# bf16 operands for the LayerNorm sums of the feed-forward phase in a two-layer transformer kernel

## The chip, the cores and the metric

The kernel runs on all 8 NeuronCores of one Trainium2 chip (trn2). Each core does the same program on its own batch element, with no exchange between cores, so there is one launch and eight equal shares. The metric is the device time of the slowest core in microseconds (us). TensorE (PE) does matmuls, VectorE (DVE) and ScalarE (ACT) do element-wise work and read the matmuls' results, SyncE (SP) and GpSimd (POOL) issue the DMAs. The engines run side by side and meet at semaphores.

## The reference, cut to what matters

For each of 8 batch elements, x is 4096 tokens by 1024 features. Two pre-norm layers are applied:

```python
x = x + attn0(layernorm(x))    # 16 heads, causal, sigmoid instead of softmax
x = x + ffn0(layernorm(x))     # silu(x @ wg.T) * (x @ wu.T) @ wd.T, hidden 3072, weights int / 127
x = x + attn1(layernorm(x))    # one head, band of 256, layernorm on its output
x = x + ffn1(layernorm(x))     # activations rounded to 8 bits, ternary weights

def _layernorm(x, axis=-1, eps=1e-5):
    m = jnp.mean(x, axis=axis, keepdims=True)
    v = jnp.var(x, axis=axis, keepdims=True)
    return (x - m) / jnp.sqrt(v + eps)
```

The change touches the mean and the variance of the layernorm in the second line.

## The kernel before

The four lines above are four phases, one after the other, with a barrier between them; they hand x on through DRAM. All of x is kept feature-major: 1024 features are 8 chunks of 128 partitions, and the 4096 tokens lie along the free axis. Phase 2 is `emit_p2`. It first loads and converts its three weight matrices, then loops over 8 blocks of 512 tokens (`NT2 = 8`, `W2 = 512`, `NDC = 8` chunks).

`emit_stats` computes a block's mean and variance. Since the features lie along the partitions, the sum over them is a matmul with a column of ones: for each of the 8 chunks ACT squares the chunk (`AF.Square`, line 96 by the helper `act`), PE adds the chunk to a row of sums and its square to a second row (both recorded at line 76, the helper `mm`). Then a few operations on one row of 512 follow: four on DVE (the first writes `r_mean`), Ln and Exp on ACT, one more on DVE. Two matmuls with a row of ones spread the two rows over 128 partitions (`ab`, `bb`). `emit_apply` multiplies by `ab` into the f32 scratch `self.sq` (shown as `sqb` in the profile) and adds `bb`, giving the normalized block in bf16, 16 DVE operations (line 123 by the helper `tt`).

`emit_stats` has two forms. Without `cast_bufs`, the sums are f32 matmuls that read x itself and an f32 square in `self.sq`. With `cast_bufs`, DVE first casts each chunk to bf16 (helper `vcopy`, line 128), ACT writes the square as bf16, and the two matmuls are bf16 with a bf16 column of ones. Each of the two scratch pairs is used in turn, and the cast and the square of chunk i wait for the matmul of chunk i - 2. Phases 1, 3 and 4 use the second form with buffers of their own; phase 2 uses the first. SBUF in phase 2 is mostly taken by the weights.

The order in each engine's queue is the order of the program text, since every engine runs its list in order. In phase 2 that is: `stage(0)` (load, statistics, apply of block 0), then for each block the 24 hidden tiles (8 gate matmuls, 8 up matmuls, Silu on ACT, product on DVE), then `stage(tc + 1)`, the statistics and the apply of the next block, then the 8 down tiles of this block. Each down tile is 24 matmuls into the one PSUM bank `Y`, and an add of the residual tile `p_xres` on DVE which also frees the bank for the next down tile; so the first such add stands behind the 16 apply operations in DVE's queue. The residual tiles and the next block of x are loaded by SP, the results stored by POOL.

Of the kernel before, what the change touches and what calls it, by code (L numbers as in the profile page):

```python
# [7 lines left out]
BF16 = mybir.dt.bfloat16  # L8
# [166 lines left out]
class Builder:  # L175
# [392 lines left out]
    def emit_p2(self):  # L568
        nc, p, d = self.nc, self.plan, self.d
        gd, sc, ve, pe = self.gd, self.sc, self.ve, self.pe  # L570
# [75 lines left out]
        src_r = src.rearrange("(c p) t -> p c t", p=128)  # L646
        dst_w = dst.rearrange("(c p) t -> p c t", p=128)

        apply_of = {}
        store_done = {}  # L650
        sil_done = {}
# [4 lines left out]
        def stage(tcn):  # L656
            lds = self.lxA
            prev_apply = apply_of.get(tcn - 1, 0)
            if tcn == 0:
                nld = tc0_ld  # L660
            else:
                p.dma("sync", x1col.ap().rearrange("p (c j) -> p c j", c=NDC),
                      src_r[:, :, tcn * W2:(tcn + 1) * W2],
                      waits=[(ve, prev_apply)], inc=lds)
                nld = lds.n
            bc = self.emit_stats(
                lambda i, b=x1col: b[:, i * W2:(i + 1) * W2], W2, NDC,
                ab, bb, [(lds, nld)],
                war_bank=[(ve, prev_apply)] if prev_apply else [])
            apply_of[tcn] = self.emit_apply(  # L670
                lambda dc, b=x1col: b[:, dc * W2:(dc + 1) * W2],
                lambda dc: xn1[:, dc * W2:(dc + 1) * W2],
                W2, NDC, ab, bb, bc)

        stage(0)
        for tc in range(NT2):
            apply_done = apply_of[tc]
# [29 lines left out]
            if tc + 1 < NT2:  # L707
                stage(tc + 1)
# [523 lines left out]
```

How the kernel before makes its waits and increments, by code:

```python
            def section(e, _ops=ops):  # L162
                for fn, wl, inc, by in _ops:
                    for s, v in wl:
                        e.wait_ge(s.h, v)
                    if fn is None:
                        continue
                    ins = fn(e)
                    if inc is not None:
                        ins.then_inc(inc.h, by)
```

## Time and profile before

| | us |
|---|---|
| median of the two timed runs | 5796.78 |
| the two runs | 5672.54, 5921.03 |
| the profiled execution | 5667.68 |
| its span on the slowest core (core 6) | 5666.1 |
| spans of the eight cores | 5641.7 to 5666.1 |

The mean granted clock of TensorE is 0.727 to 0.732 of full speed on all eight cores in the profiled execution. Phase 2 has its first matmul on x at 2063 us and its last at about 3596 us; the first 200 us of that are the loading and the conversion of the weights. Times in the rows below are us from the start of the span, unless marked ns. In a timeline row the first number is the start, the second the time from the first start to the last end of so many instructions (x2 is two of them), and the bracket gives how long the engine sat idle before it and which instruction's end let it go on. The f32 matmuls leave two records each.

### The profile page before, as it was taken

To read this page: it belongs to the slowest core of one execution; us is meant where nothing else is said; L and a number is where in the kernel's file an instruction comes from. 1 tells how busy PE (TensorE), PEld (TensorE's weight loads), DVE (VectorE), ACT (ScalarE), POOL (GpSimd) and SP (SyncE) were. 2 spreads that over 40 slices of the span, in tenths; PEclk is the share of its full clock that TensorE was granted. 3 is DMA by queue.
4 is the path that set the end of the run, shared out by engine and by line. 5 is a ranking of instruction groups with operands and counts; after the bars stand their busy time and mean duration, and the time that the engine had idled before them with its cause. 6 is when DMAs were issued, how large, how long until landed. Compare 5 with 4: busy or idle time off the path is not lost.

```text
span 5666.1 us, 48803 instructions; the slowest of 8 cores (5641.7 to 5666.1 us)
## 1 busy us (share of the span) xinstructions
PE 3582.7 (63%) x14626; PEld 1346.6 (24%) x14770; DVE 1871.3 (33%) x4451; ACT 1743.1 (31%) x1790; POOL 86.1 (2%) x150
## 2 busy tenths in 40 slices
PE   3376666766766720898888898456565556345554
PEld 0011111211111100333333333123333223111211
DVE  5613222132132210222222212134444444465555
ACT  2175665755756631211111111011111222011111
POOL 0000000000000000000000000000000000000000
PEclk6576765666767665899999999777777677556566
DMA  3100000000000054011110010400000000101010
GB/s 89 45 1 30 30 1 30 0 30 30 1 30 30 1 128 102 19 45 45 45 43 17 31 44 30 102 1 31 31 31 31 31 31 15 45 30 60 30 60 30
DMA packets 71534, 206.60 MB, mean 36 GB/s; under 512 B 5746, under 2 KB 9842, under 8 KB 69234
## 3 DMA queue, kind: packets, MB, share of 16 engines
q1 hardware_dynamic: 47474, 112.24, 6.3%
q0 software_dynamic: 23808, 91.24, 5.2%
q8 instruction: 129, 2.11, 0.2%
q14 instruction: 123, 1.01, 0.1%
HBM read 152.08 MB, written 67.11 MB: 39 GB/s over the span
## 4 chain that ended last, share of the span: by engine, by line
PE 50%; DVE 22%; ACT 14%; issue 8%; DMA 5%; DVEq 1%; ACTq 0%; SPq 0%; POOL 0%; POOLq 0%
PE pW L76 33%; PE p L76 12%; ACT p_ate L96 6%; ACT p_ato L96 5%; DVE sqb L123 3%; DVE p_xn L123 3%; PE pW L86 2%; PE p L86 2%; DVE p_ato L123 1%; DVE p_ate L123 1%; DVE p_osb L128 1%; DMA p_wq<-wqkv 1%; DMA p_wl<-w0d 1%; DVEq L165 1%; DMA p_wl<-w0g 1%
## 5 line engine op out<-in xcount | busy, mean ns | idle before, releaser
L76 PE MATMUL pW<-p_xn,p_kc 64*128 64x512 bf16 x2304 | 698.1, 502 | 287.4 <-ACT p_ato L96 142.5
L96 ACT ACTIVATE p_ate<-pW 128x1536 bf16<-128x1536 f32 (+2 forms) x408 | 560.9, 1375 | 600.7 <-PE pW L76 582.5
L96 ACT ACTIVATE p_ato<-pW 128x1536 bf16<-128x1536 f32 (+2 forms) x408 | 561.0, 1375 | 41.9 <-PE pW L76 8.1
L76 PE MATMUL p<-p_ate,p_vc 128*64 128x512 bf16 x1152 | 474.1, 544 | 135.9 <-DVE p_ato L123 135.7
L79 PE MATMUL p<-p_ato,p_vc 128*64 128x512 bf16 x1152 | 479.8, 543 | 9.0 <-ACT p_ato L96 8.2
L123 DVE TENSOR_TENSOR p_x1c<-p_xc,p 64x512 f32<-64x512 f32 x128 | 87.7, 685 | 1068.2 <-PE p L79 1061.2
L76 PE MATMUL p<-p_h,p_wd 128*128 128x512 bf16 x1504 | 369.3, 403 | 101.5 <-DVE p_xres L123 96.9
L76 PE MATMUL pW<-p_xn,p_wq 128*128 128x512 bf16 x1504 | 346.4, 392 | 128.1 <-DVE p_xn L123 93.9
L76 PE MATMUL pW<-p_xn,p_wg 128*128 128x512 bf16 x1504 | 361.4, 380 | 14.9 <-DVE p_xn L123 13.3
L76 PE MATMUL pW<-p_xn,p_wu 128*128 128x512 bf16 x1504 | 360.5, 379 | 1.7
L76 PEld LDWEIGHTS pW<-p_xn,p_kc 64*128 64x128 bf16 x2304 | 159.6, 106 | 802.2 <-issue 764.8
L123 DVE TENSOR_TENSOR p_h<-p_h,pW 128x512 bf16<-128x512 bf16 x192 | 132.1, 688 | 534.2 <-PE pW L76 509.7
L96 ACT ACTIVATE p_h<-pW 128x512 bf16<-128x512 f32 x192 | 114.6, 597 | 516.0 <-PE pW L76 515.9
L76 PEld LDWEIGHTS p<-p_ate,p_vc 128*64 128x64 bf16 x1152 | 126.0, 138 | 454.8 <-issue 441.8
L76 PEld LDWEIGHTS pW<-p_xn,p_wq 128*128 128x128 bf16 x1536 | 153.7, 100 | 329.4 <-issue 160.1
L76 PEld LDWEIGHTS p<-p_h,p_wd 128*128 128x128 bf16 x1536 | 153.3, 103 | 325.0 <-issue 176.7
L76 PE MATMUL pW<-p_xb,ones_b 128*1 128x512 bf16 x192 | 96.2, 501 | 196.0 <-DVE p_xb L128 194.6
L96 ACT ACT_TABLE_LOAD x19 | 24.4, 1283 | 584.3 <-PE pW L76 521.7
L76 PEld LDWEIGHTS pW<-p_xn,p_wg 128*128 128x128 bf16 x1536 | 150.5, 98 | 196.4 <-issue 16.1
L76 PEld LDWEIGHTS pW<-p_xn,p_wu 128*128 128x128 bf16 x1536 | 150.5, 98 | 182.0 <-issue 1.4
L76 PE MATMUL pW<-sqb,ones_col 128*1 128x512 f32 x128 | 67.1, 606 | 198.5 <-ACT sqb L96 198.5
L86 PE MATMUL pW<-ident_f,p_xn 128*128 128x128 f32 x256 | 109.2, 447 | 124.9 <-DVE p_xtm L128 99.4
(126 smaller groups left out, 3644.8 us busy)
## 6 DMA issues: line engine op xcount, KB each, us to landing
p_xc<-XIN SPq DMA_DIRECT2D x8, 2048.0 KB, 12.8
SCR<-p_x1c POOLq DMA_DIRECT2D x8, 2048.0 KB, 14.3
p_x1col<-SCR SPq DMA_DIRECT2D x8, 2048.0 KB, 12.2
p_xres<-SCR SPq DMA_DIRECT2D x64, 256.0 KB, 2.7
SCR<-p_xres POOLq DMA_DIRECT2D x64, 256.0 KB, 2.4
p_x2col<-SCR SPq DMA_DIRECT2D x8, 2048.0 KB, 10.2
SCR<-p_x2col POOLq DMA_DIRECT2D x8, 2048.0 KB, 7.9
p_x3col<-SCR SPq DMA_DIRECT2D x8, 2048.0 KB, 8.9
```

The costliest lines, as they stand in the source:

```text
L76: fn = lambda e, o=out, l=lhsT, r=rhs, s1=start, s2=stop: e.matmul(o, l, r, start=s1, stop=s2)
L79: fn = lambda e, o=out, l=lhsT, r=rhs, s1=start, s2=stop, t=tp: e.matmul(o, l, r, start=s1, stop=s2, tile_position=t)
L86: lambda e, o=out, i=in_, d=ident: e.transpose(o, i, d), waits, inc)
L96: lambda e, o=out, i=in_, f=func, k=kw: e.activation(out=o, in_=i, func=f, **k), waits, inc)
L123: lambda e, o=out, a=in0, b=in1, p=op: e.tensor_tensor(out=o, in0=a, in1=b, op=p), waits, inc, chain=chain)
L128: "vector", lambda e, o=out, i=in_: e.tensor_copy(out=o, in_=i),
L165: e.wait_ge(s.h, v)
```

## The change

Phase 2's call of `emit_stats` gets `cast_bufs`. There are no new buffers: each of the two f32 scratch tiles `self.sq` (128 x 512 f32) is seen as 1024 bf16, the first half of which takes the cast chunk and the second the square. `emit_stats` and `emit_apply` are unchanged.

```diff
@@ -646,6 +646,9 @@
         src_r = src.rearrange("(c p) t -> p c t", p=128)
         dst_w = dst.rearrange("(c p) t -> p c t", p=128)
 
+        sqbf = [self.sq[i].bitcast(BF16) for i in range(2)]
+        xbv = [sqbf[i][:, 0:512] for i in range(2)]
+        sbv = [sqbf[i][:, 512:1024] for i in range(2)]
         apply_of = {}
         store_done = {}
         sil_done = {}
@@ -666,7 +669,8 @@
             bc = self.emit_stats(
                 lambda i, b=x1col: b[:, i * W2:(i + 1) * W2], W2, NDC,
                 ab, bb, [(lds, nld)],
-                war_bank=[(ve, prev_apply)] if prev_apply else [])
+                war_bank=[(ve, prev_apply)] if prev_apply else [],
+                cast_bufs=(xbv, sbv))
             apply_of[tcn] = self.emit_apply(
                 lambda dc, b=x1col: b[:, dc * W2:(dc + 1) * W2],
                 lambda dc: xn1[:, dc * W2:(dc + 1) * W2],
```

## Rows read from the trace of the kernel before

**Rows 1.** The page's first part: engine, busy us, share of the span, instructions.

```profile
PE 3582.7 (63%) x14626; PEld 1346.6 (24%) x14770; DVE 1871.3 (33%) x4451; ACT 1743.1 (31%) x1790; POOL 86.1 (2%) x150
```

**Rows 2.** The chain of work that ended last, by engine.

```profile
PE 50%; DVE 22%; ACT 14%; issue 8%; DMA 5%; DVEq 1%; ACTq 0%; SPq 0%; POOL 0%; POOLq 0%
```

**Rows 3.** Instructions of `p_x1col`: ns min/median/max, first and last start.

```profile
L76 PE MATMUL pW<-p_x1col,ones_col x128: 590/592/1061, 2063.4 to 3398.3; 128*1 128x512 f32 x128
```

**Rows 4.** Timeline of the second call of `emit_stats` in phase 2.

```profile
2386.26 1.35 ACT L96 ACTIVATE sqb<-p_x1col 128x512 f32<-128x512 f32 x2
...
2387.08 1.02 PE L76 MATMUL pW<-p_x1col,ones_col 128*1 128x512 f32 x2
2387.33 0.69 DVE L123 TENSOR_TENSOR p_h<-p_h,pW 128x512 bf16<-128x512 bf16 x1 [2.77 <-PE pW L76]
...
2387.94 1.02 PE L76 MATMUL pW<-sqb,ones_col 128*1 128x512 f32 x2
...
2401.15 0.68 DVE L106 TENSOR_SCALAR r_mean<-pW 1x512 f32<-1x512 f32 x1 [13.14 <-PE pW L76]
```

**Rows 5.** Stretches: length, then busy PE, PEld, DVE, ACT, POOL, clock, DMA.

```profile
2387.00:2401.00 14.00, 13.97 (x33) 2.60 (x32) 0.69 (x1) 4.39 (x7) 0.00 (x0) 1.00 0.00 0
...
2424.00:2430.00 6.00, 5.39 (x15) 2.00 (x16) 0.46 (x1) 0.00 (x0) 0.55 (x1) 0.56 0.28 87
...
3625.00:3633.00 8.00, 6.43 (x16) 1.27 (x16) 3.80 (x9) 5.04 (x8) 0.00 (x0) 0.64 0.99 255
4429.00:4437.00 8.00, 5.95 (x16) 1.31 (x16) 4.24 (x10) 3.78 (x6) 0.00 (x0) 0.75 0.01 2
```

**Rows 6.** Timeline from the broadcasts to the third down tile; last row: seventh call.

```profile
2407.19 2.04 PE L76 MATMUL pW<-r_var,ones_row 1*128 1x512 f32 x2 [6.21 <-ACT r_var L96]
...
2423.78 0.69 DVE L123 TENSOR_TENSOR p_xres<-p_xres,p 128x512 f32<-128x512 f32 x1
...
2424.61 7.66 PE L76 MATMUL p<-p_h,p_wd 128*128 128x512 bf16 x24 [6.03 <-DVE p_xres L123]
...
2433.35 5.34 PE L76 MATMUL p<-p_h,p_wd 128*128 128x512 bf16 x23 [1.08 <-DVE p_xres L123]
...
3423.01 6.81 PE L76 MATMUL p<-p_h,p_wd 128*128 128x512 bf16 x24 [6.87 <-DVE p_xres L123]
```

**Rows 7.** Timeline of two calls in phase 3, which have `cast_bufs`.

```profile
3625.27 1.35 ACT L96 ACTIVATE p_sqb<-p_x2col 128x512 bf16<-128x512 f32 x2 [75.03 <-DMA p_x2col<-SCR]
3625.28 0.96 DVE L128 CAST p_xb<-p_x2col 128x512 bf16<-128x512 f32 x2 [21.85 <-DMA p_x2col<-SCR]
...
3625.85 0.59 PE L76 MATMUL p<-p_xb,ones_b 128*1 128x512 bf16 x1 [23.35 <-DVE p_xb L128]
...
3626.23 0.63 PE L76 MATMUL pW<-p_sqb,ones_b 128*1 128x512 bf16 x1
...
3627.02 0.63 ACT L96 ACTIVATE p_sqb<-p_x2col 128x512 bf16<-128x512 f32 x1 [0.39 <-PE pW L76]
...
3632.62 0.68 DVE L106 TENSOR_SCALAR r_mean<-p 1x512 f32<-1x512 f32 x1 [0.92 <-PE pW L76]
...
4432.97 2.79 ACT L96 ACTIVATE p_sqb<-p_x2col 128x512 bf16<-128x512 f32 x4 [0.28 <-PE pW L76]
...
4436.47 0.68 DVE L106 TENSOR_SCALAR r_mean<-p 1x512 f32<-1x512 f32 x1 [1.02 <-PE pW L76]
```

**Rows 8.** Timeline around the first call of `emit_stats` in phase 2.

```profile
2183.33 0.29 DVE L106 TENSOR_SCALAR p_wd<-p_wd 128x512 bf16<-128x512 bf16 x1 [1.15 <-DMA p_wd<-w0d]
...
2263.02 1.35 ACT L96 ACTIVATE sqb<-p_x1col 128x512 f32<-128x512 f32 x2
...
2265.45 1.91 PE L76 MATMUL pW<-p_x1col,ones_col 128*1 128x512 f32 x2
...
2279.53 0.68 DVE L106 TENSOR_SCALAR r_mean<-pW 1x512 f32<-1x512 f32 x1 [95.91 <-PE pW L76]
...
2302.23 3.19 PE L76 MATMUL pW<-p_xn,p_wg 128*128 128x512 bf16 x7 [13.26 <-DVE p_xn L123]
```

## Prediction

> **What bounds the kernel now.** I read the page's head first: TensorE (PE) has matmuls in 63% of the span and no other compute engine passes 33% [rows 1]. That is an average over four phases with different limits, so the chain of work that ended last comes next: half of it is PE, 22% VectorE (DVE), 14% ScalarE (ACT) [rows 2]. PE or what PE waits for sets the end. The change touches one phase only, so the rest of the reading is of that phase, the feed-forward phase 2.
>
> Then the instructions of `p_x1col`: the sums over x are 128 f32 matmul records with a median of 592 ns, the first at 2063 us and the last at 3398 us [rows 3], two records per matmul, so 64 sums in 8 calls (one per block of 512 tokens). Another 64, on the squares, read `sqb`. The timeline of one call shows how they lie [rows 4]. The records overlap: a pair starts every 0.86 us (2387.08, 2387.94), so one f32 matmul of 512 columns costs 0.86 us, and 16 of them fill the stretch from 2387.08 to 2400.8. PE has nothing else then: the gate and up products of this block are over, the down products stand behind the call in PE's queue. DVE shows a single idle time of 13.14 us that PE ends. The stretch view says the same: PE busy 13.97 of 14 us at clock 1.00, DVE 0.69, ACT 4.39 [rows 5]. So in this stretch PE alone is the limit.
>
> What follows is a chain with no slack either: four row operations on DVE, two ACT passes on one partition, two broadcast matmuls (the first at 2407.19, after 6.21 us of PE idleness), 16 apply operations on DVE, and behind them in DVE's queue the residual add of the first down tile at 2423.78 [rows 6]. PE finished that tile's 24 matmuls early and sits idle 6.03 us until the add. So whatever the sums lose or gain is passed on undiminished to 2423.78 and to everything later. The seventh and last call of this kind shows 6.87 us there [rows 6]. PE thus has 6 to 7 us in hand in its first down tile.
>
> **What the change does, part by part.** Only the call for phase 2 gets `cast_bufs`. In each of 8 calls it removes 16 f32 matmuls and puts in 8 DVE casts f32 to bf16, 16 bf16 matmuls, and lets the 8 squares be written as bf16. No DMA is added or moved; SP's and POOL's queues are untouched, and POOL is at 0.00 in this stretch [rows 5]. The scratch is the two halves of `sqb`, which DVE wrote last in the apply before (for a steady block some 125 us earlier), so the guards on it (`sq_ve_war`, `sq_war`) are long satisfied.
>
> Costs by rows. The cast: phase 3 does exactly this one, two in 0.96 us, so some 0.43 each and a gap of 0.10 [rows 7]. The square: two in 1.35 us to bf16 as to f32 [rows 4, 7], which is 0.63 each at a spacing of 0.70 to 0.72 (four in 2.79). The bf16 matmul: 0.22 us at full clock (24 in 5.34 [rows 6]); at half clock twice that, 0.43 (two f32 records span 1.91 us cold [rows 8] and 1.02 warm [rows 4], that is 0.89 more for 0.86 more of streaming). The order of the chain is new: PE must wait for the first cast, which waits in DVE's queue behind the last gate-times-up product (start 2387.33, 0.69 us, [rows 4]). Behind the casts on DVE stand only the row operations, which need the sums anyway.
>
> I lay out a steady call with t=0 at that product's start. With the gap it takes 0.79, so cast 0 starts at 0.79; the first sum starts 0.57 after its cast (3625.28 to 3625.85): 1.36. The first square sum stands 0.22 behind it and spans 0.42 (0.63 cold, less 0.21 for the faster clock): 2.00. ACT did squares 0 and 1 already and starts number 2 some 0.16 after that end (3626.86 to 3627.02) [rows 7]: 2.16. From there it is ACT-bound: six squares, 5 x 0.70 + 0.63 = 4.13: 6.29. From the end of the last square to the first row operation is 0.71 (4432.97 + 2.79 = 4435.76, to 4436.47) [rows 7]: 7.00. Before, this row operation came at 13.82 (2387.33 to 2401.15) [rows 4]. Saved: 6.82 us. Casts do not bind (0.43 in 0.70), nor does PE (two matmuls, 0.43 in 0.70).
>
> Bounds of this: the first call of phase 3, at a mean clock of 0.64 [rows 5], takes 7.34 us from cast to row operation (3625.28 to 3632.62) [rows 7]; that gives 0.79 + 7.34 = 8.13 and a saving of 5.69. The other end is the ACT-bound layout itself. I take it, because the call starts at clock 1.00 [rows 5], and a call that begins cold in phase 3 (mean clock 0.75 [rows 5]) has its last four squares back to back, ACT-bound [rows 7].
>
> The first call is different: ACT reaches it late, after the weight conversion. Squares start at 2263.02 and the row operation at 2279.53, 16.51 us, since the first pairs run at half clock [rows 8]. DVE's last weight scaling was at 2183.33 [rows 8], so casts 0 and 1 and the first sum will be long done. The first call of phase 3 needed 7.35 from first square to row operation (3625.27 to 3632.62), also cold. Saved: 9.16 us. It too lies on the path: the gate matmuls wait 13.26 us for it, up to the last apply [rows 8].
>
> Sum: seven steady calls x 6.82 = 47.7, plus 9.2: **56.9 us**. Against the profiled execution, 5667.7 us, that is **5611 us**, or 1.0% less. The two timed runs are 5672.5 and 5921.0 with a median of 5796.8; the profiled execution lies 4.8 us under the lower, so the forecast is for a run like those two.
>
> **The clock is where a gain can be given back.** As the second down tile starts, the granted clock is 0.56 [rows 5], and that tile pays for it: its 24 matmuls take 7.66 us in the first and 6.81 in the last of the seven calls, where the next tile takes 5.34 [rows 6]. That already is so, since PE idles 6.21 us before the broadcasts and 6.03 before the second tile; both idle times stay as they are, so I cost this at nothing new. If the sparser sums cost clock, the first down tile, wholly cold, is 24 x 0.43 = 10.2 us, 2.9 over the 7.3 it can have had (it ended 6.03 before 2424.61, that is at 2418.6), within the 6.03 in hand: still covered. The second tile wholly cold would be 10.2 against some 7.6 us (7.66 is taken): 2.6 us more a call, 18 us in seven. Fully warm it would be 2.3 less a call, 16 us in seven.
>
> The Trainium skill, page "TensorE: Matmul & The Clock Gate", section "A second HAM failure mode: psum-queue depth-cycling", speaks against the change: a PE that idles briefly and often between groups of matmuls swings between its two clock levels and loses throughput. By that rule the new sums would fall to half clock, as in rivals A and B, and the time would be 5619 to 5637. This trace bears it out only weakly: phase 3's sums idle in just this way, and the stretch there still has a mean clock of 0.64 and 0.75, above the lower level, after a cold start.
>
> **Rivals.**
> A. The sums run at half clock. A call then takes the 8.13 of the upper bound: saved 7 x 5.69 + 9.2 = 49.0, so 5619. For it: 1.4 us in which PE waits for the first cast and about 3.4 us of matmul in 7. Against it: the square run of phase 3 at 0.70 [rows 7].
> B. A, and the second down tile is cold too: 5619 + 18 = 5637. Against: nothing in the 10 us before that tile changes.
> C. The clock comes back sooner after the shorter call: 5611 - 16 = 5595. I see no reason beyond phase luck of the clock.
> D. The gain is hidden: something else holds the first residual add. Its other input is the `p_xres` load, which SP issues a whole gate-and-up stretch earlier for the first two tiles, and PE's idle time shows that the add came last; time 5668.
> E. Slower: the clock stays low into the down products. A cold tile in place of a warm one costs 10.2 - 5.3 = 4.9 us. To eat 56.9 us in seven calls takes 8.1 us each, more than the second tile (2.6) and the third (4.9) together; with the fourth too it is 12.4 a call, 87 in all: 5698. Against: the clock is back within the second tile, as the third's 5.34 us shows [rows 6].
>
> **How the numbers follow.** Forecast 0.62, A 0.16, B 0.07, C 0.07, D 0.04, E 0.02, and 0.02 for something that gains much more. The likeliest gives 5611. The range takes in A, B, C and the 5 us between runs: 5592 to 5645. A measurement of this kernel tells about 2% (113 us) from no change, so every case but the last falls within it: faster 0.02, same 0.96, slower 0.02.
>
> **What would show it.** In the changed profile: 128 f32 records of 592 ns on `p_x1col` gone and 64 bf16 ones in their place; DVE's one idle of 13.14 us before `r_mean` broken into short ones; ACT's squares at 0.70 spacing; `r_mean` about 7.0 us after the last product's start (8.1 if A); PE busy in the call about 6 of 7 us at a clock near 1.00 (near 0.6 if A); the second down tile still near 7 to 8 us (10 if B); PE's wait for the first residual add still 5 to 7 us; phase 3 begins 57 us earlier, at about the same length. I am wrong if the stretch from the row operation to the second tile grows, or if the other phases move.

## The result

| | kernel before | changed kernel |
|---|---|---|
| median of all runs, us | 5758.8 (10 runs) | 5617.3 (11 runs) |
| lowest, us | 5665.0 | 5606.1 |
| profiled execution, us | 5667.7 | 5632.9 |
| ratio of comparable runs | 1 | 0.9876, 95% interval 0.9817 to 0.9935 |

Some runs of either kernel are lengthened by a lower clock on the cores of one or both dies (up to 5946.7 us before, 5869.2 after); the ratio compares runs without that. The changed kernel is faster by about 1.2%, by the interval between 0.7 and 1.8%. In a second measurement (below) the ratio was 0.9845 [0.9792, 0.9898].

First the second call of `emit_stats` in phase 2, as a timeline of the changed kernel (start, length, instruction, idle time before it and what ended it), which answers to [rows 4] and [rows 6]:

```profile
2372.83 1.35 ACT L96 ACTIVATE sqb<-p_x1col 128x512 bf16<-128x512 f32 x2
2373.89 0.69 DVE L123 TENSOR_TENSOR p_h<-p_h,pW 128x512 bf16<-128x512 bf16 x1 [2.77 <-PE pW L76]
2374.68 0.96 DVE L128 CAST sqb<-p_x1col 128x512 bf16<-128x512 f32 x2
2375.26 1.12 PE L76 MATMUL pW<-sqb,ones_b 128*1 128x512 bf16 x4 [1.54 <-DVE sqb L128]
2376.06 4.24 ACT L96 ACTIVATE sqb<-p_x1col 128x512 bf16<-128x512 f32 x6 [1.88 <-PE pW L76]
...
2380.99 0.68 DVE L106 TENSOR_SCALAR r_mean<-pW 1x512 f32<-1x512 f32 x1 [1.02 <-PE pW L76]
...
2386.68 2.04 PE L76 MATMUL pW<-r_var,ones_row 1*128 1x512 f32 x2 [5.87 <-ACT r_var L96]
...
2403.27 0.69 DVE L123 TENSOR_TENSOR p_xres<-p_xres,p 128x512 f32<-128x512 f32 x1
2404.11 7.45 PE L76 MATMUL p<-p_h,p_wd 128*128 128x512 bf16 x24 [6.24 <-DVE p_xres L123]
...
2412.63 5.34 PE L76 MATMUL p<-p_h,p_wd 128*128 128x512 bf16 x23 [1.08 <-DVE p_xres L123]
```

From the last product (2373.89) to the row operation (2380.99) it is 7.10 us, 13.82 before. ACT's last six squares run in one piece, 4.24 us: they bind. Behind the row operation nothing has moved: 22.28 us to the first residual add (22.63 in the call of [rows 4] and [rows 6]; in either kernel two of the seven calls have 22.63 and the others 22.28), PE idle 6.24 us there, and the second down tile takes 7.45 us.

The stretches of the same call (length; busy PE, PEld, DVE, ACT, POOL; granted clock; DMA share and GB/s) answer to [rows 5]:

```profile
2374.00:2381.00 7.00, 5.14 (x16) 1.27 (x16) 4.00 (x10) 3.96 (x7) 0.00 (x0) 1.00 0.01 2
2381.00:2391.00 10.00, 3.99 (x5) 1.44 (x7) 3.52 (x6) 2.54 (x3) 0.00 (x0) 0.68 0.00 0
...
2404.00:2410.00 6.00, 5.89 (x18) 2.31 (x19) 0.00 (x0) 0.00 (x0) 0.55 (x1) 0.63 0.28 87
```

The sums no longer keep PE busy without a gap, and yet the clock stays at 1.00, its upper level, through them.

The first call, which answers to [rows 8]:

```profile
2259.45 1.35 ACT L96 ACTIVATE sqb<-p_x1col 128x512 bf16<-128x512 f32 x2
...
2266.74 0.68 DVE L106 TENSOR_SCALAR r_mean<-pW 1x512 f32<-1x512 f32 x1 [0.92 <-PE pW L76]
...
2289.45 3.11 PE L76 MATMUL pW<-p_xn,p_wg 128*128 128x512 bf16 x7 [13.27 <-DVE p_xn L123]
```

7.29 us from first square to row operation, 16.51 before.

Taken apart with the first and last starts of `p_x1col`, `p_xres`, `p_x2col` and `p_x3col` on each core, the program's parts are (middle values over the cores):

| part | before | changed |
|---|---|---|
| start to the load of `p_x1col` (phase 1) | 2044 | 2047 |
| first square to first apply, first call | 26.1 | 16.9 |
| first apply to last residual add (the eight blocks of phase 2) | 1313.5 | 1267.8; cores 0 and 1: 1291, 1292 |
| last residual add to first square of phase 4 | 1340 | 1336 |
| phase 4, first square to last `p_x3col` operation on DVE | 710 | 711 |

So the gain lies where the change was made, 9.2 and 45.7 us, and the rest is the same within what cores differ by. Cores 0 and 1 lost 24 us of it again in this one execution, and core 0 is the one that sets the profiled time. That loss is one place: six down tiles in a row take 7.54 us each for 6.42, and the gate-and-up stretch behind them 100.8 us for 82.8. It is seen in the granted clock of core 0 (first fence) against the same stage on core 6 (second fence, some 20 us earlier there), same columns:

```profile
2940.00:3010.00 70.00, 69.47 (x262) 28.99 (x267) 11.46 (x17) 10.15 (x17) 0.00 (x0) 0.81 0.02 4
```

```profile
2920.00:2990.00 70.00, 69.63 (x319) 31.76 (x325) 14.45 (x21) 11.94 (x20) 0.00 (x0) 1.00 0.02 5
```

Both are dense gate and up matmuls; core 0 had a clock of 0.81 and shows 262 matmul records where core 6 shows 319.

### The profile page after: what moved, and what is told of

Its sections match the earlier page's. It is cut to its first block, busy times and chain, and to the rows that moved or that the text cites. A ratio compares the mean times of both kernels' runs of the same rounds, so it can differ in the third digit from the quotient of the medians.

```text
span 5631.4 us, 48788 instructions; the slowest of 8 cores (5582.1 to 5631.4 us)
## 1 busy us (share of the span) xinstructions
PE 3535.4 (63%) x14499; PEld 1342.4 (24%) x14642; DVE 1898.1 (34%) x4515; ACT 1743.0 (31%) x1790; POOL 86.1 (2%) x150
## 4 chain that ended last, share of the span: by engine, by line
PE 50%; DVE 22%; ACT 14%; issue 8%; DMA 5%; DVEq 1%; ACTq 0%; SPq 0%; POOL 0%; POOLq 0%
PE pW L76 33%; PE p L76 12%; ACT p_ate L96 6%; ACT p_ato L96 6%; DVE sqb L123 3%; DVE p_xn L123 3%; PE pW L86 2%; PE p L86 2%; DVE p_ate L123 1%; DVE p_ato L123 1%; DVE p_osb L128 1%; DMA p_wq<-wqkv 1%; DVEq L165 1%; DMA p_wl<-w0d 1%; DMA p_wl<-w0g 1%
## 5 line engine op out<-in xcount | busy, mean ns | idle before, releaser
L76 PE MATMUL pW<-sqb,ones_b 128*1 128x512 bf16 x128 | 42.6, 404 | 237.5 <-DVE sqb L128 158.5
```

The lines of the kernel that those rows point to most:

```text
L76: fn = lambda e, o=out, l=lhsT, r=rhs, s1=start, s2=stop: e.matmul(o, l, r, start=s1, stop=s2)
```

## The experiments

My theory is the prediction's: a call's sums were bound by PE's f32 rate, become bound by ACT's squares, and the rest of the call, a chain without slack, passes the gain on; the clock is neither lost nor won. The rivals are a clock lost in the sums, a gain absorbed by a later wait, and another bound of the new call. All times of phase 2 below are from first apply to last residual add, 1313.5 before and 1267.8 changed.

### The changed kernel once more

> The changed kernel itself, beside the kernel before on one chip in five rounds, for the size of the gain alone. By the prediction's sum, 56.9 us of 5667.7 or 0.9900 of before. Its parts as first measured, 9.2 us in the first call and 46 in the seven others, give 55 us, 0.9903. Rival (the change also costs clock somewhere, or gains in the other phases): phases 1, 3 and 4 move by more than the 10 us by which cores differ, or the ratio lies outside 0.988 to 0.993.

Measured: median 5614.1 us of 6 runs, ratio 0.9845 [0.9792, 0.9898]; the profiled execution 5609.7. On all eight cores the first call is 16.5 to 16.9 us and the eight blocks 1266.0 to 1268.0; phase 1 takes 2038 to 2053, phase 4 709 to 711. The parts are as first measured, and without the clock loss of cores 0 and 1 the profiled execution is within 2 us of the predicted 5611. The ratio's middle lies outside the 0.988 to 0.993 that I gave; its interval reaches to 0.9898 and takes in part of it. Ten of the eleven runs of before on that chip were at 5678 us or above, where on another chip nine of thirteen lay between 5665 and 5674. So I take it that the ratio's other side is what moved; no profile of before on that chip shows it. The parts say 55 us, or 0.990.

### Only the first call

```diff
-                cast_bufs=(xbv, sbv))
+                cast_bufs=(xbv, sbv) if tcn == 0 else None)
```

> Only the first of phase 2's eight calls has the bf16 form; the other seven are f32 as before. My theory (each call's saving passes undiminished to the end, and the calls are independent): first square to first apply 16.9 us as in the changed kernel against 26.1 before, the seven f32 calls back at 13.8 us from the last product to the row operation, the rest of phase 2 at 1313.5 us as before. 9.2 us in all, about 5659 beside 5668, ratio about 0.998. Rival (the saving is absorbed by a later wait, or the first call's gain needs the others): phase 2 as long as before, or the seven calls shorter than 13.8 without having been changed.

Measured: the first call 16.5 to 17.2 us on all cores, the seven others 13.82 or 13.83 us from last product to row operation, the eight blocks 1311.8 to 1316.8. The calls are independent and the first is worth 9.2 us. The ratio, 0.9999 [0.9960, 1.0039], takes in the expected 0.998 and no change alike; only the profile can tell 9 us here. The profiled execution took 5654.3.

### More buffers for the casts and squares

```diff
-        xbv = [sqbf[i][:, 0:512] for i in range(2)]
-        sbv = [sqbf[i][:, 512:1024] for i in range(2)]
+        xbv = [xn1[:, i * 512:(i + 1) * 512] for i in range(8)]
+        sbv = [sqbf[i // 2][:, (i % 2) * 512:(i % 2 + 1) * 512] for i in range(4)]
```

(Cut to the buffers. The first call keeps the two pairs, and the waits in `emit_stats` change with the buffers: in the other calls no cast waits for a matmul, and the square of chunk i waits for that of chunk i - 4.)

> The changed kernel, but in its seven steady calls the eight casts go to the eight chunks of p2_xn1, which is free then, and the squares to four bf16 halves of sqb, so that no cast waits for a matmul and four squares can run before the first cast. My theory (the call is bound by ACT's squares, the first two of which are early, the third waiting for the first pair of matmuls): with four squares early the run of squares ends sooner, some 1.1 us less per call, last product to row operation near 6.0 us instead of 7.1, 8 us in seven calls: 5604 beside the changed kernel's 5612. Rival 1 (the call is bound by the chain cast, matmul, matmul at PE's pace): still 7.1 us. Rival 2 (casts are the bound): casts at 0.53 us spacing end at 0.79 + 4.2 = 5.0, row operation at 5.9, which can't be told from my theory by the time but by the order of the last square and the last cast.

Measured: 5.84 or 5.85 us from last product to row operation in all or all but one of the seven calls of each core (the odd one 5.92), 7.10 in the changed kernel, so rival 1 (a chain at PE's pace) is out. The timeline of the second call on core 2:

```profile
2381.00 2.80 ACT L96 ACTIVATE sqb<-p_x1col 128x512 bf16<-128x512 f32 x4
2382.06 0.69 DVE L123 TENSOR_TENSOR p_h<-p_h,pW 128x512 bf16<-128x512 bf16 x1 [2.77 <-PE pW L76]
2382.85 4.14 DVE L128 CAST p_xn<-p_x1col 128x512 bf16<-128x512 f32 x8
...
2384.22 2.80 ACT L96 ACTIVATE sqb<-p_x1col 128x512 bf16<-128x512 f32 x4 [0.42 <-PE pW L76]
...
2387.90 0.68 DVE L106 TENSOR_SCALAR r_mean<-pW 1x512 f32<-1x512 f32 x1 [0.92 <-PE pW L76]
```

The squares end at 2387.02 and the casts at 2386.99, so ACT and DVE now bind together, as rival 2 had it; one cannot say which. In the changed kernel, where the casts end 0.3 us ahead of the squares, the two-deep scratch put ACT's third square behind the first pair of matmuls, and that cost 1.26 us a call.

The time is another matter. On cores 4 to 7 the eight blocks took 1255.1 to 1256.5, 12 us less than the changed kernel, where 1.26 x 7 = 8.8 were due. Another 1.1 is three down tiles that take 6.78 us in the changed kernel and 6.42 here, and some 2 us are the second down tiles, which wander. On cores 0 to 3 they took 1265.0 to 1267.6: nothing gained. There the gate and up matmuls of the next block show why, on core 2:

```profile
2462.82 2.27 PE L76 MATMUL pW<-p_xn,p_wu 128*128 128x512 bf16 x8
2464.92 2.27 PE L76 MATMUL pW<-p_xn,p_wg 128*128 128x512 bf16 x8
...
2468.91 1.89 PE L76 MATMUL pW<-p_xn,p_wg 128*128 128x512 bf16 x8
```

For some 6 us, eight matmuls start every 2.10 us instead of 1.73. The granted clock of the stretch from 2460 to 2470 is 0.87 to 0.89 on cores 2 and 3 and 1.00 on cores 4 to 7; cores 0 and 1 had 0.89 in the 10 us before. The gate-and-up stretch behind the first eight down tiles is 83.9 us on core 2 and 82.8 on core 5, and the six after it are alike: 7.3 to 7.7 us lost in seven on cores 0 to 3. The run's time, 5615.2 in the profile, and the others up to 5768.5 give no comparison.

### PE kept busy in its idle times

```diff
+        def fill1():
+            for _ in range(26):
+                p.mm(self.p7[:, 0:512], wg[:, 0:128], wu[:, 0:512], True, True)
+        def fill2():
+            for _ in range(30):
+                p.mm(self.p7[:, 0:512], wd[:, 0:128], hcol[:, 0:512], True, True)
```

(`fill1` is called behind the sums of the seven steady calls, `fill2` behind the first down tile; both write a PSUM bank that nothing reads.)

> The changed kernel with useless bf16 matmuls of constants into an unused PSUM bank in PE's two idle times of each steady call: 26 after the sums (5.7 us warm) and 30 behind the first down tile (6.5 us warm). They add nothing to the output. My theory of the clock (the idle times cost the clock, and the second down tile pays for it with 1.4 to 3 us): broadcasts at full clock, 1.7 us less from row operation to first apply, the second down tile 5.34 us instead of 6.8 to 8.3, so 22.3 us from row operation to the first residual add become 20.6, and to the second add 31.3 become 27.2. About 4 us a call, 28 in seven: 5584. Rival (the clock drop in the second tile has nothing to do with PE's idleness, or comes only from it in the 10 us before): both stretches as in the changed kernel, or the fillers stand in the way and the time grows by up to 2 us a call: 5612 to 5626.

Measured: ratio 0.9857 [0.9837, 0.9876], median 5592.0 us. Six cores have 1239.3 to 1239.8 us for the eight blocks, 28.2 less than the changed kernel. Cores 2 and 3 have 1247; six of their seven gate-and-up stretches take 83.9 us for 82.8, as with more buffers. A call on core 3:

```profile
2385.68 5.79 PE L76 MATMUL p<-p_wu,p_wg 128*128 128x512 bf16 x26
...
2391.61 1.09 PE L76 MATMUL pW<-r_var,ones_row 1*128 1x512 f32 x2
...
2393.50 12.41 PE L76 MATMUL p<-p_h,p_wd 128*128 128x512 bf16 x54
...
2407.25 5.34 PE L76 MATMUL p<-p_h,p_wd 128*128 128x512 bf16 x24 [1.34 <-DVE p_xres L123]
```

The broadcast's two records span 1.09 us, 2.04 before; the row operation is 20.48 us ahead of the first residual add (2385.93 to 2406.41), not 22.28; and the second down tile takes 5.34 us. PE's idleness is what cost the clock, and the low clock cost 28 us in all, as worked out from the rows: 7 x 1.80 = 12.6 at the broadcasts, the rest in the second down tile. Work that is thrown away pays for itself here.

### The statistics inside the gate and up loop

The next block's casts, squares, sums, row operations and broadcasts go into the loop over hidden tiles; only the apply stays behind it.

```diff
             for ht in range(24):
+                if nxt is not None and 9 <= ht <= 12:
+                    sum_pair(nxt, ht - 9)      # 4 matmuls
+                if nxt is not None and ht == 16:
+                    bcast()
 ...
+                    if 8 <= ht <= 11:
+                        cast_pair(nxt, ht - 8) # 2 casts, 2 squares
```

(Cut. The row operations, Ln and Exp, and the last row operation stand behind tiles 12, 13 and 14.)

> The changed kernel, but for blocks 1 to 7 the whole statistics of the next block (casts, squares, sums, row operations, broadcasts) stand inside the gate and up loop, hidden tiles 8 to 16, where DVE and ACT idle 3 us of every 3.45; only the 16 apply operations stay behind the last product. My theory (the stretch from last product to first residual add is a chain with no slack, whatever engine it is on): that stretch goes from 7.1 + 22.3 = 29.4 to 0.8 + 12.7 = 13.5 us, 15.9 less a call, 111 in seven; the matmuls moved into the loop cost PE 3.5 + 1.7 us a call, 37 in seven; net 74: 5538. Rival (ACT's two more table loads and Ln/Exp in the loop stall the gate tiles): the loop grows by 2 to 4 us more a call, and the net is 50 to 60: 5555 to 5562.

Measured: 1246.7 to 1249.1 us for the eight blocks on cores 2 to 7, only 20 less than the changed kernel, and a ratio of 0.9909 [0.9872, 0.9946]. (Cores 0 and 1 had 1252 and 1255, and 1386 and 1388 us in phase 3, where the others had 1339 to 1350; the change touches nothing there. The clock of core 0 over that stretch is 0.68, of core 2 0.70.) The stretch behind the loop was as expected: PE now waits 8.47 us for the residual add. What I had missed is in the loop, here on core 2:

```profile
2498.54 0.69 DVE L123 TENSOR_TENSOR p_h<-p_h,pW 128x512 bf16<-128x512 bf16 x1 [4.47 <-PE pW L76]
2499.33 0.96 DVE L128 CAST sqb<-p_x1col 128x512 bf16<-128x512 f32 x2
2499.90 1.12 PE L76 MATMUL pW<-sqb,ones_b 128*1 128x512 bf16 x4 [1.54 <-DVE sqb L128]
...
2506.12 1.12 PE L76 MATMUL pW<-sqb,ones_b 128*1 128x512 bf16 x4 [1.54 <-DVE sqb L128]
```

The four sums of a pair of chunks come every 6.22 us, where a hidden tile takes 3.45: 2.77 us a pair, 11 a call of the 13 by which the loop grows. Of it 1.54 is PE's wait for the first cast, which stands behind the product of the tile that PE has only just finished; in the queue of an in-order PE everything behind waits too. The table loads, my rival's cause, stall nothing.

### The sums two tiles later

```diff
-                if nxt is not None and 9 <= ht <= 12:
-                    sum_pair(nxt, ht - 9)
+                if nxt is not None and ht in (8, 10, 12, 14):
+                    sum_pair(nxt, (ht - 8) // 2)
-                    if 8 <= ht <= 11:
-                        cast_pair(nxt, ht - 8)
+                    if ht in (6, 8, 10, 12):
+                        cast_pair(nxt, (ht - 6) // 2)
```

(Cut. The row operations and the broadcasts move two tiles back with the sums. The pairs also stand two tiles apart now, so two things change at once.)

> As e6_stats_in_loop, but each pair of chunks is cast in hidden tile 6, 8, 10 or 12 and its sums stand two tiles later in PE's queue instead of one. In e6 the loop grew by 13 us a call: each pair of sums stood directly behind the tile whose product DVE does before the casts, so PE waited 1.54 us and each pair cost 2.8 us. My theory: with the sums later PE never waits for a cast, the pairs cost only their streaming, 3.5 us a call, and the broadcasts 1.9; the loop grows by 5.4 us, and the period of a block goes from 160.0 (changed kernel) and 157.2 (e6) to 149.6; phase 2 behind its first call from 1267.6 to about 1195: 5540 us. Rival (what made the loop longer in e6 was the matmuls themselves or the two table loads): the period stays near 157.

Measured: median 5553.9 us, ratio 0.9753 [0.9682, 0.9824]; the eight blocks take 1198.0 to 1201.3 us, 68 less than the changed kernel (73 expected), and the period of a block is 150.0 (2357.66 to 2507.62). The waits of PE from 2300 to 3330 us on core 2, which takes in all seven calls (total, times, longest), no longer name the casts, on which PE waited 43.4 us in 29 times, at most 1.5, in the same stretch of the run above:

```profile
PE p L76 <- DVE p_xres L123: 100.0, 46, 8.5
PE p L76 <- DVE p_h L123: 7.1, 7, 1.0
```

### The apply spread over the down tiles

```diff
+            if nxt is not None:
+                apply_chunk(0)
 ...
                 evac_done[dt] = ve.n
+                if nxt is not None and dt < 7:
+                    apply_chunk(dt + 1)
```

> As f6, but the 16 apply operations no longer stand together ahead of the first residual add: one chunk (two operations) stands there, and one behind each of the first seven adds, where DVE idles 5.7 us. My theory (the first down tile's add waits for the apply in DVE's queue, and PE with it): last product to first add from 13.5 to about 6.2 us, PE idle 1.1 instead of 8.5 us, so its clock is kept and the second tile takes 5.34: about 8.8 us less a call than f6, 62 in seven: 5478. Rival (the spread applies delay the adds or the next block's gate matmuls): the tiles' period grows from 6.42 by up to 1.6 us, and the gain is lost.

Measured: median 5479.4 us, ratio 0.9598 [0.9535, 0.9662]; the eight blocks 1132.3 to 1133.5 us, 67 less than with the sums moved (62 expected). PE's waits from 2300 to 3330 us, slowest core:

```profile
PE p L76 <- DVE p_xres L123: 53.2, 49, 1.4
PE p L76 <- DVE p_h L123: 7.1, 7, 1.0
```

The longest wait falls from 8.5 to 1.4 us, and the second down tile takes 5.34 us: with the idleness the low clock is gone, without any filler (granted clock 1.00 from 2300 to 3300 us, 0.94 in the changed kernel on core 2).

### A second bank for the down tiles

```diff
-        Y = self.p6[:, 0:512]
+        Yb = [self.p6[:, 0:512], self.p7[:, 0:512]]
 ...
-                pdt = dt - 1 if dt >= 1 else (7 if tc > 0 else None)
+                Y = Yb[dt % 2]
+                pdt = dt - 2 if dt >= 2 else (6 + dt if tc > 0 else None)
```

> As f7, with a second PSUM bank (unused in phase 2 before) for the down tiles in turn, so that a tile need not wait for the add of the one before. My theory: the 1.08 us of PE idleness ahead of each down tile goes, period 5.2 instead of 6.42 us, 1.1 x 63 = 70 us: 5408. Rival (the store and load of the residual tile, two buffers, take over as the limit): period between 5.3 and 6.4, 5410 to 5478.

Measured: the eight blocks 1062.8 to 1063.7 us, 69.5 less (70 expected), 5.18 us from one residual add to the next; profiled 5413.0 us, median 5433.8 of 5 runs, ratio 0.9497 [0.9433, 0.9562]. The page's first line, and the one wait above 1 us in total that PE has from 2300 to 3330 us:

```profile
span 5411.5 us, 48640 instructions; the slowest of 8 cores (5392.1 to 5411.5 us)
```

```profile
PE p L76 <- DVE p_h L123: 8.1, 8, 1.0
```

In that stretch PE is then the limit. This version beats both kernels: 5.0% less than the kernel before, of which the change studied here is 1.0 to 1.2.

## Why the prediction was right or wrong

**Right.** The time: 5611 us was predicted, the medians were 5617 and 5614, all inside 5592 to 5645. Step by step:

- The bound before was PE's f32 streaming. Taken away, the call shrank to what ACT allows.
- The first call, 9.16 us: measured 9.2.
- A steady call, 7.00 us from product to row operation: measured 7.04 to 7.19, mean 7.10 on core 0 and 7.08 on others. Square 2 starts 2.17 us after the product (2376.06), as laid out. The one term that was mis-sized is the run of six squares: 4.24 us, not 4.13, because I took a spacing of 0.70 where the row that I cited for it (four in 2.79) gives 0.72.
- The gain is passed on: 22.3 us from row operation to residual add before and after, PE's wait at that add still 6.24 us. Rival D is out.
- Sum: 56.9 predicted, 55 measured (9.2 + 45.7). The saving per steady call was 13.78 - 7.10 = 6.68 and not 6.82, for the reason just given and because one of the calls before was at 13.48 and not 13.82; the 1.1 us that are left are three of the 48 down tiles behind the second ones, which take 6.78 us for 6.42 on every core of the changed kernel. Why, no run shows.
- The clock: 1.00 through the sums, so A and B are out. C, a second tile that is warm, did not happen by itself; the run with useless matmuls shows that it would have needed PE to be busy, and what it is then worth (28 us, of which 15.6 in the second tile, where I had counted 16, and 12.6 at the broadcasts, which I had not counted).
- The clock did fall where PE sat idle for 5.9 and 6.2 us: to 0.68 in the 10 us from the row operation to the broadcasts and 0.63 at the second down tile. Both were there before.
- The rule of the Trainium skill that the prediction cites (page "TensorE: Matmul & The Clock Gate", section "A second HAM failure mode: psum-queue depth-cycling"), on a PE that idles briefly between groups of matmuls, did not show in these sums: 5.14 us of matmuls in 7, at full clock.

**Wrong.** Two steps failed.

The first is the anchoring: "the forecast is for a run like those two". One of the two runs, 5921.0 us, lies 253 us above the execution that the terms were made from, and the median 5796.8 is half made of it. Read against that median, as the sentence invites, 5611 is a fall of 3.2%, when the sum says 1.0% and the measurement 1.2%. The runs since taken of the kernel before show how little one time stands for it: three of ten lie within 20 us of 5667.7, the other seven at 5741 to 5947. The terms were made against 5667.7 and are good only against it: the sentence should have named 5672.5 alone as comparable and given the ratio, 0.990.

The second is the resolution. I wrote that a measurement of this kernel tells about 2% from no change, and so put 0.96 on no change that counts. The interval of the ratio was [0.9817, 0.9935], half a width of 0.6%, and does not hold 1. The prediction gave no run for the 2%, only the two times 4% apart. On another chip nine of thirteen runs of the kernel before lie within 0.2%, so a gain of 1.0% can be measured; the forecast should have said "faster by 1%, and measurably".

## What to carry to other kernels

When a stretch is a chain without slack, its gain is simply the difference of the chain laid out from rows, latencies between engines included; the work is in finding what the new chain is bound by, here ACT, the engine beside the one that was relieved. Before making such a stretch cheaper, ask whether it has to stand on the path: the cheaper sums were worth 46 us in seven calls, moving them and the apply under other matmuls another 134. But in an in-order queue a moved instruction needs its operands ready when it arrives; one tile too early cost 48 us of phase 2 (1248 against 1200). And make a forecast's sum and its ratio against one and the same execution.

## What the runs showed of the hardware

- Dense matmuls on all eight cores are at times granted a clock between the two levels: 0.81 on cores 0 and 1 for some 150 us (262 matmul records in 70 us where core 6 has 319), or some 6 us at a time on all four cores of the first die. It came on pairs of cores of the first die in the runs profiled, and cost 24 us in one execution and, on those four cores, the gain of more buffers in another. The Trainium skill, page "TensorE: Matmul & The Clock Gate", section "Seeing it yourself", has a level of 13/16 (1.95 GHz, 0.81 of full) for a whole die once three of its cores run dense matmuls. The level agrees with the 0.81 here; that it takes a whole die at once does not, since from 2940 to 3010 us cores 2 and 3 had 1.00 to the other two's 0.81. What sets it off no run here shows.
- Useless matmuls in idle times of 6 us made phase 2 of this kernel 28 us shorter on six of eight cores (1239.6 for 1267.8); the medians, 5592 to 5614 or 5617, were taken on different chips.
- Back to back, squares of 128 x 512 come every 0.72 us (six in 4.24) and casts to bf16 every 0.53 (eight in 4.14), although a square is 0.63 long and a cast 0.43: a gap of some 0.10 us between one operation's end and the next one's start is part of the price.
